# The last attention of a four-layer kernel: masking and exp in PSUM, probabilities as two 16-bit parts, turned by DMA instead of TensorE

## Chip, cores and metric

The kernel runs on one core of a Trainium2 chip. The metric is the time of one execution on the device in microseconds; the median of several runs is compared. TensorE, VectorE (DVE), ScalarE (ACT), GpSimd (POOL) and SyncE (SP) each work through an order of their own and wait for each other by semaphores. Every matmul writes to one of eight PSUM banks of 128 x 512 floats.

## What is computed

Four layers, each a cross attention and a feed-forward block with residuals, on x of 512 tokens by 512. The change touches only the attention of the last layer (B = 2 batches, 256 queries, 512 keys, 32 heads of 16 with 8 key groups, and a mask of true and false):

```python
def _L3_xattn_ref(q, k, v, w_q, w_k, w_v, w_out, mask):
    query = q @ w_q.T; key = k @ w_k.T; value = v @ w_v.T
    ...
    scores = jnp.einsum('bghnd,bgsd->bghns', query, key) / D_HEAD ** 0.5
    scores = jnp.where(mask, scores, jnp.finfo(scores.dtype).min)
    attention = jax.nn.softmax(scores, axis=-1)
    out = jnp.einsum('bghns,bgsd->bghnd', attention, value)
    return out.transpose(0, 3, 1, 2, 4).reshape(b, n, D_MODEL) @ w_out.T
x = x + _L3_xattn_ref(_layernorm(x), ctx_4096, ctx_4096, ..., mask_SxS2_bk0)
x = x + _L3_ffn_ref(_layernorm(x), ...)
```

## The kernel before

All arithmetic is to hold 32-bit accuracy, so operands are split into a high and a low part and multiplied part by part. The layers follow each other on every engine; layernorm ln6 leads into the last attention (`l3_...`), ln7 into the last feed-forward block (`f3_...`).

The last attention works on 128 tiles, each the scores of 128 queries against 512 keys for one head. `l3_tile(i)` gives a tile's block (four blocks of 32 tiles: batch and half of the heads), its head and its half of the queries; four tiles are a quad, and the two tiles of one head in a quad are a unit. The work is laid out in slots: slot k runs from -7 to 135, and each engine's function walks through the slots in the same order and does in slot k what is due there.

- TensorE (`l3_pe`): `scores` computes two tiles at a time (four matmuls, L1866) into the four banks `ring` (named ps_s in the profile); tile i has `ring[i % 4]`, and the bank is free when its mask is done (semaphore max). Two slots later `l3_pe` turns the tile's probabilities, four transposes of 128 x 128 (L1911), into `ps_t[0]` or `ps_t[1]` by turns; `take_turn_bank` waits until both parts of the piece before have left the bank. Turned values and turned reciprocals of the sums take turns in the same two banks; `pieces3` lists all pieces in order. `attend` (L1880) multiplies values and turned probabilities of a unit, eight matmuls, the unit's last tile four slots before. Projections (`l3_project`, `jobs3`) stand between them: a query job in 12 of the 32 quads, a key, value or output job in 10, none in 10. They use `ps_t[2]`.
- VectorE (`l3_dve`): in slot k `largest` adds the mask to tile k, takes the row maximum and writes the masked scores to SBUF (`l3p`, six buffers, L1995); then it forms the low part of the turned probabilities of tile k - 3 (L2019).
- ScalarE (`l3_act`): in slot k it copies the high part of the turned tile k - 3 (L1953), then takes exp of tile k in SBUF (L1962) with the row sums.
- GpSimd (`l3_pool`) splits weights, spreads reciprocals (L1789) and splits the attention's output (L1802, L1804).
- SP (`l3_sp`, `f3_sp`) issues the DMAs, each behind its wait, in one queue; in this stage only loads of weights, 8.4 MB.

```python
e.wait_ge(s3["exp"], i + 1)
for kk in range(4):
    mm = e.transpose(o[:, kk * P:(kk + 1) * P], l3p[:, i % 6, kk * P:(kk + 1) * P], ident[:, :])
mm.then_inc(s3["T"], 1)
```

The first attention (`L0`, class functions at L1220 to L1345) already works as the change does: masked scores and exp stay in PSUM (L1274, L1247), ScalarE writes a first 16-bit part (L1220), VectorE the second (L1315), and a DMA transpose turns both (L1071), one tile every 3.4 us.

## Time and profile before

| | |
|---|---|
| median of 3 runs | 1912.69 us (1910.24 to 1915.45) |
| the profiled execution, its own time | 1909.78 us |
| its span, first to last instruction | 1908.0 us |
| TensorE matmul, busy | 1752.3 us, 92% |
| TensorE weight load | 1419.0 us, 74% |
| VectorE | 1422.7 us, 75% |
| ScalarE | 1049.8 us, 55% |
| GpSimd | 882.7 us, 46% |
| mean granted TensorE clock | 0.972 of 2.4 GHz |
| DMA | 226.13 MB, mean 119 GB/s |

Busy shares are over the whole span, which has eight blocks with different limits; the last attention is its part from 1514 to about 1753 us. A line number names the operation in the code. In the groups, the time behind the bar is the idle time of the engine just before the operation, and behind it what ended most of that.

### The profile page before, as it was taken

To read this page: it belongs to the slowest core of one execution; us is meant where nothing else is said; L and a number is where in the kernel's file an instruction comes from. 1 tells how busy PE (TensorE), PEld (TensorE's weight loads), DVE (VectorE), ACT (ScalarE), POOL (GpSimd) and SP (SyncE) were. 2 spreads that over 40 slices of the span, in tenths; PEclk is the share of its full clock that TensorE was granted. 3 is DMA by queue.
4 is the path that set the end of the run, shared out by engine and by line. 5 is a ranking of instruction groups with operands and counts; after the bars stand their busy time and mean duration, and the time that the engine had idled before them with its cause. 6 is when DMAs were issued, how large, how long until landed. Compare 5 with 4: busy or idle time off the path is not lost.

```text
span 1908.0 us, 28955 instructions
## 1 busy us (share of the span) xinstructions
PE 1752.3 (92%) x9892; PEld 1419.0 (74%) x9892; DVE 1422.7 (75%) x3036; ACT 1049.8 (55%) x1999; POOL 882.7 (46%) x863
## 2 busy tenths in 40 slices
PE   6899999999797999978899999999988999998988
PEld 5677777777576888757688888888866778776755
DVE  6777887878577887747677777778755587787898
ACT  5766667666125565631556556656641287775333
POOL 6776776664633232044343444343336632242762
PEclk9999999999899999998999999999998999998998
DMA  5656656565417999651589778889762200120210
GB/s 183 142 103 139 134 116 141 121 120 118 121 25 141 213 194 175 136 121 50 108 159 196 160 166 175 164 162 194 149 141 78 75 1 23 46 90 22 73 44 23
DMA packets 524177, 226.13 MB, mean 119 GB/s; under 512 B 493696, under 2 KB 503168, under 8 KB 516736
## 3 DMA queue, kind: packets, MB, share of 16 engines
q1 hardware_dynamic: 524032, 224.28, 53.9%
q8 instruction: 81, 1.33, 0.3%
q14 instruction: 64, 0.52, 0.1%
HBM read 97.08 MB, written 5.24 MB: 54 GB/s over the span
## 4 chain that ended last, share of the span: by engine, by line
PE 69%; DVE 17%; DMA 3%; ACT 3%; issue 3%; POOL 3%; SPq 1%; POOLq 0%; DVEq 0%; ACTq 0%
PE ps_t L339 9%; PE ps_t L340 8%; PE ps_t L341 8%; PE ps_s L339 8%; PE ps_s L340 7%; PE ps_s L341 7%; PE ps_o L339 4%; PE ps_o L340 3%; PE ps_o L341 3%; PE ps_o L1880 3%; PE ps_t L1911 3%; ACT ps_s L1247 2%; PE ps_s L1866 2%; DVE nmax L1277 2%; DVE ps_s L1274 1%
## 5 line engine op out<-in xcount | busy, mean ns | idle before, releaser
L1247 ACT ACTIVATE ps_s<-ps_s,nmax 128x768 f32<-128x768 f32 (+1 forms) x320 | 252.6, 789 | 342.0 <-DVE nmax L1277 239.5
L1220 ACT ACTIVATE l_ab<-ps_s,rinv 128x768 f16<-128x768 f32 (+1 forms) x320 | 260.8, 815 | 69.0 <-DVE rinv L1322 54.1
L1315 DVE SCALAR_TENSOR_TENSOR l_ab<-ps_s,rinv,l_ab 128x768 f16<-128x768 f32 (+1 forms) x320 | 289.1, 903 | 2.8 <-ACT l_ab L1220 2.4
L1277 DVE TENSOR_REDUCE nmax<-ps_s 128x1 f32<-128x768 f32 x192 | 183.5, 956 | 123.3 <-PE ps_s L341 122.9
L339 PE MATMUL ps_o<-l_pt,l_v 128*128 128x256 f16 (+1 forms) x832 | 230.9, 278 | 19.3 <-DMA l_v<-l_vab 9.2
L340 PE MATMUL ps_o<-l_pt,l_v 128*128 128x256 f16 (+1 forms) x832 | 229.6, 276 | 0.0
L341 PE MATMUL ps_o<-l_pt,l_v 128*128 128x256 f16 (+1 forms) x832 | 229.5, 276 | 0.0
L339 PE MATMUL ps_s<-l_k_hi,l_q_hi 128*128 128x512 f32 (+3 forms) x512 | 186.4, 364 | 21.9 <-DVE l_ab L1315 18.9
L377 POOL TENSOR_TENSOR wo_hi<-raw_big,one 128x512 fp32r<-128x512 f32 (+2 forms) x100 | 103.8, 1038 | 204.6 <-PE ps_t L341 123.6
L340 PE MATMUL ps_s<-l_k_lo,l_q_hi 128*128 128x512 f32 (+3 forms) x512 | 179.8, 351 | 0.0
L341 PE MATMUL ps_s<-l_k_hi,l_q_lo 128*128 128x512 f32 (+3 forms) x512 | 179.1, 350 | 0.0
L377 POOL TENSOR_TENSOR wq_hi<-raw_big,one 128x512 fp32r<-128x512 f32 (+1 forms) x100 | 103.5, 1035 | 123.5 <-PE ps_t L341 59.2
L339 PEld LDWEIGHTS ps_s<-l_k_hi,l_q_hi 128*128 128x128 f32 (+1 forms) x512 | 96.4, 188 | 60.9 <-DVE l_ab L1315 32.2
L379 POOL TENSOR_TENSOR wq_lo<-raw_big,wq_hi 128x512 fp32r<-128x512 f32 (+1 forms) x100 | 127.5, 1275 | 7.8
L683 POOL TENSOR_TENSOR w_raw<-w_raw,w_row 128x512 f32<-128x512 f32 x32 | 41.1, 1285 | 191.4 <-DMA w_raw<-in_f_w 191.4
L2019 DVE TENSOR_TENSOR l_pt_lo<-ps_t,l_pt_hi 128x512 fp32r<-128x512 f32 x128 | 88.4, 691 | 48.2 <-ACT l_pt_hi L1953 45.5
L379 POOL TENSOR_TENSOR wo_lo<-raw_big,wo_hi 128x512 fp32r<-128x512 f32 (+2 forms) x100 | 120.7, 1207 | 7.8
L1274 DVE CUSTOM_DVE_ANT_0 ps_s<-ps_s,l_mask 128x512 f32<-128x512 f32 x128 | 88.7, 693 | 46.9 <-PE ps_s L341 46.9
L339 PEld LDWEIGHTS ps_o<-l_pt,l_v 128*128 128x128 f16 (+1 forms) x832 | 87.1, 105 | 48.0 <-issue 29.4
L339 PE MATMUL ps_t<-xT_hi,wq_hi 128*128 128x512 f32 (+1 forms) x296 | 117.1, 396 | 3.5 <-DVE xT_lo L2136 2.7
L340 PE MATMUL ps_t<-xT_lo,wq_hi 128*128 128x512 f32 (+1 forms) x296 | 110.9, 375 | 0.0
L341 PE MATMUL ps_t<-xT_hi,wq_lo 128*128 128x512 f32 (+1 forms) x296 | 110.7, 374 | 0.0
(386 smaller groups left out, 4947.0 us busy)
## 6 DMA issues: line engine op xcount, KB each, us to landing
raw_big<-in_l_wq SPq DMA_DIRECT2D x18, 1024.0 KB, 5.9
raw_big<-in_l_wo SPq DMA_DIRECT2D x18, 1024.0 KB, 5.9
w_raw<-in_f_w SPq DMA_DIRECT2D x32, 256.0 KB, 3.6
raw_big<-in_f_w SPq DMA_DIRECT2D x7, 1024.0 KB, 4.9
raw_kv<-in_l_wkv SPq DMA_DIRECT2D x12, 512.0 KB, 6.5
l_pt<-l_ab SPq DMA_TRANSPOSE x320, 3.7
raw_f<-in_f_w SPq DMA_DIRECT2D x4, 1024.0 KB, 4.8
w_nat<-in_f_w1n SPq DMA_DIRECT2D x16, 256.0 KB, 3.9
```

The costliest lines, as they stand in the source:

```text
L339: pe.matmul(o, a[0], b[0], start=start, stop=False)
L340: pe.matmul(o, a[0], b[1], start=False, stop=False)
L341: return pe.matmul(o, a[1], b[0], start=False, stop=stop)
L377: pool.tensor_tensor(hi, w, one[0:parts, 0:1].to_broadcast([parts, cols]), ALU.mult).then_inc(w_rdy[role], 1)
L379: pool.tensor_tensor(lo, w, hi.bitcast(F32), ALU.subtract).then_inc(w_rdy[role], 1)
L1220: e.activation(sp.ab[:, (k - 1) % 3, 0, :], self.scores_out(k - 1), ACT.Copy, scale=rinv[:, i:i + 1]).then_inc(s_pa, 1)
L1247: e.activation(self.scores_out(k), self.scores_out(k), ACT.Exp, bias=nmax[:, i:i + 1], scale=-1.0 if l.rope else 1.0, accum_out=rsum[:, i: ...
L1274: e.tensor_tensor_reduce(out=o, in0=o, in1=sp.mask[:, 2 * b + qt, :], scale=-1.0, scalar=F32_MAX, op0=ALU.add, op1=ALU.min, accum_out=nmax ...
L1277: e.tensor_reduce(nmax[:, i:i + 1], o, AX.X, ALU.max, negate=True).then_inc(s_max, 1)
L1315: e.scalar_tensor_tensor(out=b, in0=self.scores_out(t), scalar=rinv[:, i:i + 1], in1=a, op0=ALU.mult, op1=ALU.subtract).then_inc(s_pb, 1)
L1880: mm = e.matmul(ps_o[:, 0:SQ], l3v[blk % 2][:, k, g * P:(g + 1) * P], l3pt[u % 2][y][:, k, :], start=g == 0 and k == 0 and y == 0, stop=g ...
L2019: e.tensor_tensor(pt[1], ps_t[p % 2][:, :].rearrange("p (k q) -> p k q", q=P), pt[0].bitcast(F32), ALU.subtract).then_inc(s3["tlo"], 1)
```

## The change

- The masked scores and exp stay in the scores' PSUM banks; the mask writes in place. Scores now have five banks (`l3_bank`: the four of `ring` and `ps_t[0]`), and a bank is free when the second part of its tile is out.
- ScalarE copies the first 16-bit part of tile k right behind its exp in slot k, scaled by P_SCALE; VectorE forms the second part of tile k in slot k + 1. Both go to `l3ab`, six buffers of 128 x 1024 16-bit values.
- SP issues one `dma_start_transpose` per tile, 128 in all, into `l3pt`, six units. The transposes stand in SP's queue between the loads; the first loads of the next block move into this loop, behind tiles 71, 87 and 101. `l3ab[i % 6]` is free for tile i + 6 when its transpose has landed.
- `attend` waits for the transposes of its two tiles and runs three slots later; the steps behind it move three slots as well, and the stage ends at slot 138. The 32-bit transposes on TensorE are gone, and with them `take_turn_bank` and `pieces3`; values and reciprocals alone are turned there, in `ps_t[1]` (`take_aside`).
- The values are 16-bit in two parts too, scaled by their largest magnitude: a maximum, a diagonal, one more matmul, and five short operations per batch. The scale comes off with the reciprocals.
- Projection jobs inside quads start at the third slot of a quad, not the first.

```diff
-        l3pt = [[at(f"l3_pt{i}_{n}", [P, 4, SQ], F32R, R0 + 8 + 8 * i + 4 * j) for j, n in enumerate(("hi", "lo"))]
-                for i in range(2)]
-        l3p = at("l3_p", [P, 6, SK], F32, R0 + 24)
+        l3pt = [at(f"l3_pt{i}", [P, 2, 8, P], F16, R0 + 8 + 4 * i) for i in range(6)]
+        l3ab = [at(f"l3_ab{i}", [P, 2, SK], F16, R0 + kb) for i, kb in enumerate((66, 68, 70, 72, 32, 34))]
...
-                job(kind, blk, i, 4 * quad, 4 * quad, 4 * quad + 1, 4 * quad + 1)
+                job(kind, blk, i, 4 * quad + 2, 4 * quad + 2, 4 * quad + 3, 4 * quad + 3)
...
+        def l3_bank(i):
+            return (ring[0], ring[1], ring[2], ring[3], ps_t[0][:, :])[i % 5]
...
         def l3_sp(e):
-            load(e, "q", c3.q + 1, A["l3_wq"][1], ("o", c3.o + 1))
-            load(e, "o", c3.o + 1, A["l3_wo"][1], ("q", c3.q + 2))
+            for k in range(1, N3 + 1):
+                i = k - 1
+                u = l3_unit(i)
+                e.wait_ge(s3["second_part"], i + 1)
+                if u >= 6:
+                    e.wait_ge(s3["pv"], u - 5)
+                e.dma_start_transpose(l3pt[u % 6][:, l3_tile(i)[3], :, :], l3ab[i % 6][:, :, :].rearrange("p a n -> p (a n)"))\
+                    .then_inc(s3_crossed[i % 6], 16)
+                if k == 10:
+                    load(e, "q", c3.q + 1, A["l3_wq"][1], ("o", c3.o + 1))
+                if k == 40:
+                    load(e, "o", c3.o + 1, A["l3_wo"][1], ("q", c3.q + 2))
+                if k in F3_LOADS_AT:
+                    f3_sp_ahead(e, F3_LOADS_AT.index(k))
...
             def scores(quad, qt):
-                if quad:
-                    e.wait_ge(s3["max"], 4 * quad - 2 + 2 * qt)
+                pair = 2 * quad + qt
+                if pair >= 2:
+                    e.wait_ge(s3["second_part"], 2 * pair - 3)
...
             def attend(u):
-                e.wait_ge(s3["tlo"], lo_count3[piece_at3["t", u // 2 * 4 + 2 + u % 2]])
+                for i in (u // 2 * 4 + u % 2, u // 2 * 4 + u % 2 + 2):
+                    e.wait_ge(s3_crossed[i % 6], 16 * (i // 6 + 1))
...
-                if k % 4 >= 2 and 0 <= k - 6 < N3:
-                    attend((k - 6) // 4 * 2 + k % 2)
+                if k % 4 in (1, 2) and 0 <= k - 9 < N3:
+                    attend((k - 9) // 4 * 2 + (k - 1) % 4)
...
         def l3_act(e):
-                    e.activation(l3p[:, k % 6, :], l3p[:, k % 6, :], ACT.Exp, bias=nmax[:, c:c + 1], scale=-1.0,
-                                 accum_out=rsum[:, c:c + 1]).then_inc(s3["exp"], 1)
+                    o = l3_bank(k)
+                    e.activation(o, o, ACT.Exp, bias=nmax[:, c:c + 1], scale=-1.0, accum_out=rsum[:, c:c + 1]).then_inc(s3["exp"], 1)
+                    if k >= 6:
+                        e.wait_ge(s3_crossed[k % 6], 16 * (k // 6))
+                    e.wait_ge(s3["exp"], k + 1)
+                    e.activation(l3ab[k % 6][:, 0, :], o, ACT.Copy, scale=P_SCALE).then_inc(s3["first_part"], 1)
...
         def l3_dve(e, link):
+                if 0 <= k - 1 < N3:
+                    i = k - 1
+                    a, b = (l3ab[i % 6][:, part, :] for part in (0, 1))
+                    e.wait_ge(s3["first_part"], i + 1)
+                    e.scalar_tensor_tensor(out=b, in0=l3_bank(i), scalar=P_SCALE, in1=a, op0=ALU.mult, op1=ALU.subtract)\
+                        .then_inc(s3["second_part"], 1)
...
+        F3_LOADS_AT = (72, 88, 102)
+        def f3_sp_ahead(e, step):
+            if step == 0:
...
+                for i in range(2):
+                    e.dma_start(q_w1[i][:, :, :], w1_ints[:, 2 * i:2 * i + 2, :]).then_inc(s_wback[0], 16)
+            elif step == 1:
+                e.wait_ge(w_rdy["o"], 8 * cf.o)
+                f3_load_chunk(e, 0)
+                e.dma_start(q_w2[:, :, :], w2_ints).then_inc(s_wback[1], 16)
+            else:
+                e.wait_ge(w_rdy["q"], 8 * (cf.q + 1))
+                f3_load_chunk(e, 1)
```

TensorE in a quad with a query projection, before (ps_s and ps_t are banks, l_y keys, l_x queries, l_p the probabilities to be turned):

```order
L1911 MATMUL ps_t<-ident,l_p 128x128 x4
L1866 MATMUL ps_s<-l_y_hi,l_x_116 128x512
L1866 MATMUL ps_s<-l_y_lo,l_x_116 128x512
L1866 MATMUL ps_s<-l_y_hi,l_x_116 128x512
L1866 MATMUL ps_s<-l_y_lo,l_x_116 128x512
L339 MATMUL ps_t<-xT_hi,wq_hi 128x256
L340 MATMUL ps_t<-xT_lo,wq_hi 128x256
L341 MATMUL ps_t<-xT_hi,wq_lo 128x256
L339 MATMUL ps_t<-xT_hi,wq_hi 128x256
L340 MATMUL ps_t<-xT_lo,wq_hi 128x256
L341 MATMUL ps_t<-xT_hi,wq_lo 128x256
L1911 MATMUL ps_t<-ident,l_p 128x128 x4
```

and in the change, in a quad of the same kind, where l_pt are turned probabilities and l_v values:

```order
L1887 MATMUL ps_t<-l_y_hi,l_x_116 128x512
L1887 MATMUL ps_t<-l_y_lo,l_x_116 128x512
L1887 MATMUL ps_s<-l_y_hi,l_x_116 128x512
L1887 MATMUL ps_s<-l_y_lo,l_x_116 128x512
L1902 MATMUL ps_o<-l_pt_121,l_v_140 128x256 x8
L1887 MATMUL ps_s<-l_y_hi,l_x_116 128x512
L1887 MATMUL ps_s<-l_y_lo,l_x_116 128x512
L1887 MATMUL ps_s<-l_y_hi,l_x_116 128x512
L1887 MATMUL ps_s<-l_y_lo,l_x_116 128x512
L1902 MATMUL ps_o<-l_pt_122,l_v_140 128x256 x8
L345 MATMUL ps_t<-xT_hi,wq_hi 128x256
```

The transposes of l_p are gone from between the others, two scores of every five tiles in turn go to ps_t, and each quad has its two groups of products beside the scores.

ScalarE, before, with the semaphores that each row waits for:

```order
L1953 ACTIVATE l_pt_hi<-ps_t 128x4x128 [waits l3_pv,l3_T]
L1962 ACTIVATE l_p,rsum<-l_p,nmax 128x512 [waits l3_rec,l3_max]
L1953 ACTIVATE l_pt_hi<-ps_t 128x4x128 [waits l3_pv,l3_T]
L1926 ACTIVATE l_t<-ps_t,l_selq 128x256 [waits l3_job_out,l3_job_full]
L1962 ACTIVATE l_p,rsum<-l_p,nmax 128x512 [waits l3_rec,l3_max]
L1953 ACTIVATE l_pt_hi<-ps_t 128x4x128 [waits l3_pv,l3_T]
```

and in the change:

```order
L1976 ACTIVATE ps_s,rsum<-ps_s,nmax 128x512 [waits l3_rec,l3_max]
L1980 ACTIVATE l_ab_128<-ps_s 128x512 [waits l3_exp,l3_probs_crossed_5]
L1947 ACTIVATE l_t<-ps_t,l_selq 128x256 [waits l3_job_out,l3_job_full]
L1976 ACTIVATE ps_s,rsum<-ps_s,nmax 128x512 [waits l3_rec,l3_max]
L1980 ACTIVATE l_ab_123<-ps_s 128x512 [waits l3_exp,l3_probs_crossed_0]
```

The copy of a turned tile three slots back (L1953) has become the first part of the same tile, right behind its exp, and waits for that exp and for the transpose of six tiles before.

SP's queue in the change, around the loads behind tile 87; before, the two loads stood there alone:

```order
L1758 DMA_TRANSPOSE l_pt_117<-l_ab_125 128x8x128 [waits l3_pv,l3_second_part]
L1758 DMA_TRANSPOSE l_pt_118<-l_ab_126 128x8x128 [waits l3_pv,l3_second_part]
L2093 DMA raw_big<-in_f_w 128x2048 [waits w_o_split]
L2107 DMA q_w_189<-second_weight_rounded 128x8192
L1758 DMA_TRANSPOSE l_pt_119<-l_ab_127 128x8x128 [waits l3_pv,l3_second_part]
L1758 DMA_TRANSPOSE l_pt_120<-l_ab_128 128x8x128 [waits l3_pv,l3_second_part]
```

Each transpose waits for its tile's second part and for a unit's products; the loads stand in line between them.

## Rows read from the trace of the kernel before

**Rows 1.** Stretches: busy PE, PEld, DVE, ACT, POOL, clock, DMA share, GB/s
```profile
1634.00:1694.00 60.00, 58.83 (x428) 47.81 (x429) 47.69 (x117) 47.11 (x111) 24.97 (x31) 1.00 0.23 89
...
1742.00:1760.00 18.00, 14.61 (x84) 12.65 (x84) 8.49 (x18) 3.97 (x9) 3.37 (x6) 0.88 0.00 0
```

**Rows 2.** Chain that ended last, from 1505: start us, us, engine, tile, line
```profile
1562.33 0.66 PE ps_s L1866 x4
...
1568.47 0.66 PE ps_s L1866 x4
...
1604.99 0.66 PE ps_s L1866 x4
...
1611.96 0.67 PE ps_s L1866 x4
...
1615.16 0.44 PE ps_t L1911 x4
...
1649.20 0.66 PE ps_s L1866 x3
...
1657.55 0.66 PE ps_s L1866 x4
```

**Rows 3.** Groups by form, 1514 to 1738: busy us, mean ns, idle before
```profile
L2019 DVE TENSOR_TENSOR l_pt_lo<-ps_t,l_pt_hi 128x512 fp32r<-128x512 f32 x121 | 83.6, 691 | 44.6 <-ACT l_pt_hi L1953 42.0
...
L1953 ACT ACTIVATE l_pt_hi<-ps_t 128x512 fp32r<-128x512 f32 x121 | 72.0, 595 | 46.1 <-PE ps_t L1911 43.7
```

**Rows 4.** VectorE in order of time in the last attention
```profile
1653.68 0.69 DVE L2019 TENSOR_TENSOR l_pt_lo<-ps_t,l_pt_hi 128x512 fp32r<-128x512 f32 x1
1654.29 0.42 DVE L2034 TENSOR_TENSOR l_o<-ps_o,l_r 128x256 f32<-128x256 f32 x1
```

**Rows 5.** All engines in order of time, a tile of the first attention
```profile
231.93 0.70 DVE L1274 CUSTOM_DVE_ANT_0 ps_s<-ps_s,l_mask 128x512 f32<-128x512 f32 x1 [0.47 <-PE ps_s L341]
...
232.55 0.14 DVE L1274 DVE_READ_ACCUMULATOR2_ANT nmax<- 128x1 f32 x1
232.55 0.75 DVE L1315 SCALAR_TENSOR_TENSOR l_ab<-ps_s,rinv,l_ab 128x512 f16<-128x512 f32 x1
...
232.73 0.66 ACT L1247 ACTIVATE ps_s<-ps_s,nmax 128x512 f32<-128x512 f32 x1 [1.45 <-DVE nmax L1274]
...
233.31 0.19 ACT L1247 ACTIVATION_READ_ACCUMULATOR ps_s<-ps_s,nmax 128x1 f32 x1
```

**Rows 6.** Groups by form, ScalarE, whole span
```profile
L1220 ACT ACTIVATE l_ab<-ps_s,rinv 128x512 f16<-128x512 f32 x128 | 87.7, 685 | 17.6 <-DVE rinv L1322 14.7 <-DMA l_pt<-l_ab 0.3
```

**Rows 7.** ScalarE in order of time: a pair whose second waits for the first
```profile
1886.20 0.63 ACT L2283 ACTIVATE q_c<-q_c 128x512 f32<-128x512 f32 x1 [2.81 <-DVE q_c L2376]
1886.86 0.63 ACT L2285 ACTIVATE hq<-q_c 128x512 bf16<-128x512 f32 x1
```

**Rows 8.** DMA queues, 420 to 440: packets, MB, share of 16 engines
```profile
q1 hardware_dynamic: 5784, 1.44, 37.4%
```

**Rows 9.** The transposes of the first attention, 100 to 300: issue and landing
```profile
L1071 SPq DMA_TRANSPOSE l_pt<-l_ab x55: 1231/1232/2171, 101.2 to 298.0; - x55
...
DMA to landing us min/median/max: 3.0/3.0/6.8
```

**Rows 10.** DMA queues, 1300 to 1350
```profile
DMA packets 24957, 8.71 MB, mean 174 GB/s; under 512 B 23672, under 2 KB 24312, under 8 KB 24825
...
q1 hardware_dynamic: 24953, 8.65, 88.3%
```

**Rows 11.** DMA queues, 1514 to 1742, the last attention
```profile
q1 hardware_dynamic: 1152, 8.40, 10.0%
```

**Rows 12.** VectorE in order of time: the last mask, the last scaling
```profile
1742.40 0.68 DVE L1995 CUSTOM_DVE_ANT_0 l_p<-ps_s,l_mask 128x512 f32<-128x512 f32 x1
...
1751.31 0.42 DVE L2034 TENSOR_TENSOR l_o<-ps_o,l_r 128x256 f32<-128x256 f32 x1 [2.00 <-PE ps_o L1880]
```

More of the change, by code:

```diff
@@ L1654, in program @@
         c3 = START["l3"]
-        s3 = {n: sem(f"l3_{n}") for n in ("S", "max", "exp", "rec", "T", "thi", "tlo", "pv", "spread", "scaled", "ohi", "olo", "zero", "sel",
+        s3 = {n: sem(f"l3_{n}") for n in ("S", "max", "exp", "first_part", "second_part", "rec", "aside", "aside_free", "vhi",
+                                         "vdiag", "vscale", "pv", "spread", "scaled", "ohi", "olo", "zero", "sel",
                                          "job_full", "job_hi", "job_out")}
+        s3_crossed = [sem(f"l3_probs_crossed_{i}") for i in range(6)]
         N3 = 4 * 32
@@ L1704, in program @@
         find3 = {(j.kind, j.blk, j.i): j for j in jobs3}
-        slots3 = range(-7, 136)
+        slots3 = range(-7, 139)
         steps3, ended3 = {}, {}
@@ L1811, in l3_project @@
                 e.wait_ge(s3["job_out"], {4: 0, 5: 1, L3_JOBS - 1: j.n - 1}.get(j.n, j.n) or 1)
+            if part == 0 and j.n == L3_JOBS - 1:
+                e.wait_ge(s3["second_part"], N3)
             o = j.bank()
@@ L1928, in l3_act @@
             e.wait_ge(s3["sel"], 1)
-            e.wait_ge(s3["zero"], 2)
+            e.wait_ge(s3["zero"], 3)
             job_out(jobs3[0])
@@ L2003, in l3_dve @@
             for k in slots3:
[L2004 removed]
+                if k == 124:
                     norms[7].dve_scale(e, 0)
```

180 lines of the change are left out of this document (86 added, 94 removed).

## Prediction

> **What bounds the kernel now.** I read the slices of the page first, then busy time by stretch, the chain of waits, the groups, and the engines in order of time where the change cuts in. The last attention takes its 128 tiles, by the first and last mask, from 1514.6 to 1742.4: 228 us, 1.78 us a tile, 7.12 us a quad (four tiles).
>
> In a stretch of 60 us TensorE is busy 58.8 us at its full clock of 2.4 GHz, VectorE 47.7, ScalarE 47.1, the DMA engines 23% with loads [rows 1]. The chain is TensorE's line after line, and it dates the quads: from one first pair of scores to the next it is 6.14 us in a quad without a projection, 6.97 with a query projection, 8.35 with a key, value or output projection [rows 2]. The program has 10, 12 and 10 of these: 61.4 + 83.6 + 83.5 = 228.5 us, the whole stage. VectorE and ScalarE stand idle before the two parts of the turned probabilities, 44.6 and 46.1 us in all, for each other and for TensorE's turn [rows 3]. So TensorE's order is the bound, with a good fifth of the other two free.
>
> **What goes.** The 128 groups of four TensorE transposes cost 0.44 us each on the chain [rows 2]: 128 x 0.44 = 56 us, 1.76 a quad. Left on TensorE: 4.4, 5.2 and 6.6 us by kind of quad, 172 us in all. The 16-bit products stream as many columns as the 32-bit ones; I give them no gain.
>
> **What takes its place: the loop of ScalarE and VectorE.** VectorE masks tile k and then forms the second part of tile k-1; ScalarE takes exp of k and then the first part of k. That closes a loop over two tiles: second part of k-1, mask of k+1, exp of k+1, first part of k+1, second part of k+1. Its steps, where all is ready: second part to the next operation 0.61 [rows 4]; mask to the end of its accumulator read 0.76 (231.93 to 232.69), to exp 0.04, exp to the end of its read 0.77 [rows 5]; the wait of ScalarE for itself 0.03 [rows 7]; the first part 0.60, which is the old copy out of PSUM [rows 3] (0.69 if it behaves as the first attention's, which takes its factor from memory [rows 6]; the new factor is a constant, so I take 0.60); to VectorE 0.03. Sum 2.84 us (2.93), so 1.42 a tile, 5.7 a quad. Neither engine alone is slower than that: VectorE needs 0.62 + 0.61 = 1.23 a tile, and exp with its read, wait and copy 1.40 on ScalarE.
>
> Beside these run keys, queries, scales and residuals. Today they make up what is left of VectorE's time: 47.7 us over 33.7 tiles is 1.42, less 1.23 is 0.19 a tile [rows 1, 4, 5]; for ScalarE I estimate half of that, 0.10, by its narrower copies. Put wholly into the loop they give 1.71 a tile (219 us), wholly absorbed 1.42 (182). Two such loops run interleaved, of the odd and the even tiles, and an operation put into one delays the other less, by what is left of the slack between the engines' 1.23 and 1.40 and the loop's 1.42; that is little, so I take 0.21 of the 0.29: 1.63 a tile, **209 us**, against 228: **-19**. Heavy quads need 6.6 us of TensorE against 6.5 of the loop: even, no term.
>
> **The DMA engines.** Now 128 transposes of 256 KB pass them. In a stretch with nothing else 5784 packets took 37.4% of 20 us; one transpose is 1024 packets of 256 bytes, so 7.48 / 5.65 = 1.32 us each [rows 8]. The stage's own loads, 8.40 MB, took 10.0% of 228 us, 22.8 us, 2.7 us a MB [rows 11]. Together 169 + 23 = 192 us of 209: hidden on average, but 92% full. Issue takes 1.23 us of SP's queue per transpose, landing 3.0 [rows 9]; 1.23 is under 1.63, so the queue keeps up.
>
> What it costs are the loads that sit in the same queue ahead of transposes: 2 MB behind tile 71, 3 MB behind tile 87, 1 MB behind 9, 39 and 101. The first part of tile k waits until tile k-6 has crossed. From the end of the second part of k-6 to that point are six tiles less the 2.2 us from its exp to that end, plus 0.8 to the copy: 9.8 - 2.2 + 0.8 = 8.4 us, 5.4 more than the landing takes. 1 MB (2.7 us) and 2 MB (5.4) fit, 3 MB (8.1) leave 2.7 us; with SP held at tile 101 by POOL's splitting of the query weights I take **+4**. The products on TensorE tolerate more (a unit is taken three slots later, about 10 us behind its last second part). If the cover were gone, each transpose would show its 3.0 us of landing at once: 384 us.
>
> The Trainium skill (DMA: Bandwidth & Descriptors, Latency and other measured facts) gives a DMA transpose 261 GB/s, an estimated 1.0 us for 256 KB, by which the engines would be some 150 us busy and no stall would be left; the trace gives 1.32, and that is used.
>
> **Small edits.** At the start VectorE gets a maximum over the values and five short scale operations between query results, partly beside TensorE: +1 (0 to 2). At the end the last mask starts at 1742.40 and the last scaling at 1751.31, 8.9 us [rows 12]. The new path from the last mask is 0.80, 0.77, 0.63 and 0.03, second part 0.7, landing 3.0, one product group 0.95: 6.9, plus queue delay of perhaps 1: -1 (-2 to +3). The new masks write PSUM: 0.70 for 0.68, in the steps above. Smaller zero fills on POOL lie ahead of everything: nothing.
>
> **Sum.** -19 + 4 + 1 - 1 = -15 us. The profiled execution took 1909.8 us; the median of the runs is 1912.7, 2.9 more. 1912.7 - 15 = 1897.7, so **1898 us**.
>
> **Rivals.**
> *The DMA engines become the bound, and it is slower.* Where transposes and loads are dense, they take longer: 88.3% of 50 us, less 7.0 us for 2.59 MB that were not transposes (8.65 MB less 23672 packets of 256 bytes), is 37.1 us for 23.1 units of 1024 packets, 1.61 each [rows 10]. Then the stage is 128 x 1.61 + 22.8 = 229 us, plus some 4 us before the first transpose can start and 5 of backlog behind the last mask: +8, **1921 us**. It decides from (209 - 22.8) / 128 = 1.45 us per transpose on, and is slower than before from about 1.54. For it: the load is denser than anywhere in the first attention. Against: much of the busy time in such stretches is packets waiting for each other, and the bare cost was 1.32. Chance 0.18.
>
> The Trainium skill (VectorE: DVE Perf Modes, The three transpose paths) speaks against the change in the same way, and harder: a 128 x 128 block 1309 ns by DMA against 390 ns on TensorE. Eight blocks one after the other would be an estimated 10.5 us per tile, 1340 us for the stage. The trace doesn't agree, since a transpose of eight blocks lands in 3.0 us.
>
> *Half a gain.* First part at 0.69, extras wholly in the loop and 4 us more of stalls: 1.76 a tile, 225 us: -3 + 4 = about +1, **1913 us**. VectorE's wait times support it, the length of six buffers speaks against the stalls. Chance 0.14.
>
> *More than forecast.* Extras absorbed: 1.45 a tile is 186 us, under the DMA floor of 192, so about 195 us: -33, **1880 us**. Chance 0.08.
>
> *The clock falls* between TensorE's bursts: it was 0.88 of 2.4 GHz on average where it ran thin at the end of the stage [rows 1]. At 1.2 GHz a plain quad would take 8.8 us, 2 more than now forecast; but the new gaps are under 1 us, and the low stretch had one of 3. Within the next case's width; chance 0.03, +3 us.
>
> **Numbers.** My case, 1885 to 1906 us, has 0.57; it makes nearly all of faster. Differences over 0.3% (5.7 us) can be told from none. Faster 0.67, within 0.3% 0.16, slower 0.17. The range takes in the absorbed extras and most of the DMA case: 1882 to 1920.
>
> **What would show it.** Right: TensorE 75 to 85% busy in the stage; VectorE's idle time before the second part waiting for ScalarE, hardly for TensorE; transposes landing in 3 to 5 us, a few ScalarE copies waiting for a transpose near tile 93; DMA share 0.9. Wrong: landing times that grow through the whole stage and a share of 1.0 throughout (the DMA case), or a tile over 1.75 us with short landings (the loop).

## The result and the profile after

The change makes the kernel slower: 1926.05 us median of 4 runs (1925.10 to 1928.26) against 1913.53 us of 4 runs of the kernel before (1910.24 to 1915.45) on the same chip. The ratio is 1.0070, 95% interval 1.0053 to 1.0088: **+12.5 us**, where 1898 us was forecast (1882 to 1920). The first row of each of the next two views is the stretch from the last low part of the turned layernorm ahead of the stage (`xT_lo`) to the first one of the block behind it.

Busy time by stretch, the kernel before (length; PE, PEld, DVE, ACT, POOL; clock, DMA share, GB/s):

```profile
1506.62:1762.74 256.12, 242.13 (x1676) 195.22 (x1674) 196.39 (x474) 183.22 (x428) 75.55 (x107) 0.98 0.10 35
```

The same, the changed kernel, and four stretches of 20 us inside it:

```profile
1512.45:1780.06 267.61, 211.30 (x1168) 143.59 (x1166) 208.99 (x489) 185.56 (x428) 74.08 (x107) 0.82 0.82 158
...
1554.00:1574.00 20.00, 16.11 (x121) 11.59 (x120) 18.61 (x47) 18.24 (x45) 4.11 (x8) 1.00 1.12 183
1574.00:1594.00 20.00, 15.54 (x78) 9.89 (x78) 14.46 (x33) 14.03 (x33) 11.14 (x12) 0.74 0.81 154
...
1594.00:1614.00 20.00, 17.56 (x83) 11.54 (x83) 15.42 (x36) 14.14 (x33) 2.35 (x5) 0.74 0.94 182
...
1694.00:1714.00 20.00, 14.17 (x72) 8.79 (x70) 14.64 (x35) 14.24 (x34) 11.11 (x12) 0.71 1.05 221
```

The stage is 11.5 us longer, which is most of the 12.5. (The two profiled executions themselves lie 18.5 us apart, 1928.26 and 1909.78: 5.8 us of that are ahead of the stage and 1.1 behind it. The stage begins anywhere from 1506.3 to 1516.1 in the profiled executions of the changed kernels below, whose work ahead of it is the same, so the 5.8 are taken for scatter.) TensorE's mean granted clock there went from 0.98 to 0.82 of 2.4 GHz. The clock has two levels, 1.0 and 0.5, so 0.18 / 0.5 = 36% of the stage, 96 us, ran at 1.2 GHz; before it was some 10 us. Where the clock stayed at 1.00 (1554 to 1574), VectorE and ScalarE are busy 18.6 and 18.2 of 20 us: that is the loop of the forecast. Where it was 0.71 to 0.74 they are busy 14 to 15. The DMA share adds up packet times and reaches 1.12 here, so 1.0 is not its ceiling.

Where the 11.5 us lie (times from VectorE in order of time):

| part | before | changed | forecast of the difference |
|---|---|---|---|
| last `xT_lo` to the first mask | 8.0 | 11.3 (+3.3) | +1 |
| first to last mask (127 tiles on) | 227.8 | 235.2 (+7.4) | -15 |
| last mask to the next block's `xT_lo` | 20.3 | 21.2 (+0.8) | -1 |

**The operations cost what was forecast.** Groups by form of the changed kernel, 1514 to 1745 (busy us, mean ns, idle before and its releasers):

```profile
L2033 DVE SCALAR_TENSOR_TENSOR l_ab<-ps_s,l_ab 128x512 f16<-128x512 f32 x95 | 65.6, 691 | 11.2 <-ACT l_ab L1980 10.1
L1976 ACT ACTIVATE ps_s<-ps_s,nmax 128x512 f32<-128x512 f32 x96 | 63.5, 662 | 18.9 <-PE ps_t L347 11.4 <-DVE nmax L2016 5.6
L1980 ACT ACTIVATE l_ab<-ps_s 128x512 f16<-128x512 f32 x95 | 56.7, 597 | 8.4
```

Second part 691 ns, exp 662, first part 597 (I took 0.60). The surprise is the releaser of exp: a projection's last matmul (`ps_t L347`).

**The quads give it away.** From the first mask of a quad to that of the next there are 31 intervals. A projection's result is taken by ScalarE and VectorE at the start of the quad behind it, so ten intervals hold a key, value or output result: the 2nd, 3rd, 10th, 12th, 13th, 18th, 20th, 21st, 28th and 30th. They take 10.2, 8.4, 12.0, 10.5, 6.5, 8.3, 10.3, 6.5, 9.6 and 10.3 us (rounded), 92.6 in all. At my 1.63 a tile they would be 65.2. The 24th (9.7) and the 26th (9.1) stand beside the 3 MB of loads and GpSimd's splitting of the query weights; the other 19 take 119.6, 6.3 each, *less* than the 6.5 of the forecast. My 1.63 a tile and 4 us of stalls make 211 us of the 127 tiles from first to last mask; it took 235.2. Of these 24 us, 27.4 are in the ten intervals, 1.8 in the loads' two beyond the 4 I had given them, and the rest came out 5 better. Part of the ten is no wait at all: VectorE alone is busy 67.6 us in them, 6.8 each, since the work on a projection's result falls on these quads and I had spread it evenly over all tiles.

What one of them looks like, the 10th, 1585.3 to 1597.3. The changed kernel in order of time, PE and ACT and DVE rows only:

```profile
1584.75 1.91 PE L1902 MATMUL ps_o<-l_pt,l_v 128*128 128x256 f16 x8
...
1586.31 0.77 PE L345 MATMUL ps_t<-cT_hi,wkv_hi 128*128 128x512 f32 x1
...
1590.59 0.40 PE L347 MATMUL ps_t<-cT_hi,wkv_lo 128*128 128x512 f32 x1
...
1591.02 0.60 ACT L1943 ACTIVATE l_y_hi<-ps_t 128x512 fp32r<-128x512 f32 x1 [4.29 <-PE ps_t L347]
...
1591.65 0.69 DVE L1987 TENSOR_TENSOR l_y_lo<-ps_t,l_y_hi 128x512 fp32r<-128x512 f32 x1 [4.20 <-ACT l_y_hi L1943]
...
1591.98 1.05 PE L1902 MATMUL ps_o<-l_pt,l_v 128*128 128x256 f16 x8
```

And its clock, busy time by stretch of the changed kernel:

```profile
1573.00:1576.00 3.00, 2.00 (x16) 1.15 (x14) 2.72 (x7) 2.72 (x8) 0.00 (x0) 1.00 1.01 193
1576.00:1579.00 3.00, 1.71 (x12) 1.03 (x12) 2.79 (x7) 2.75 (x7) 0.00 (x0) 1.00 1.02 190
1579.00:1585.00 6.00, 4.64 (x20) 2.42 (x21) 5.59 (x15) 4.94 (x13) 5.17 (x7) 0.56 0.98 188
1585.00:1591.00 6.00, 6.00 (x22) 4.37 (x20) 1.72 (x4) 1.64 (x4) 5.77 (x6) 0.59 0.86 164
1591.00:1597.00 6.00, 3.74 (x28) 2.26 (x28) 5.14 (x12) 5.54 (x13) 0.20 (x1) 0.98 0.43 26
```

TensorE was busy 1.7 to 2.0 of 3 us in plain quads, then the clock fell to 1.2 GHz. Eight products took 1.91 us in place of 1.05; TensorE waited 0.54 us for the spread reciprocals of GpSimd; the key projection ran from 1586.31 to 1590.99, 4.7 us. (The projection's last three matmuls, from 1590.13 on, are at full clock again.) Its result is due in ScalarE's queue ahead of the next exp, and in VectorE's ahead of the next mask: both stood still for over 4 us (busy 1.6 and 1.7 of 6). Meanwhile TensorE worked without a gap and the clock came back. The Trainium skill (TensorE: Matmul & The Clock Gate, A second HAM failure mode: psum-queue depth-cycling) tells of such an oscillation where TensorE idles briefly and often between groups of matmuls; this trace agrees, and the gaps are short ones here too (rows of them stand in the section on the prediction).

All such waits of ScalarE and VectorE, the changed kernel, 1514 to 1750 and 1516 to 1760 (engine, line, waited for: us in total, times, longest):

```profile
ACT ps_s L1976 <- PE ps_t L347: 11.4, 5, 3.9
ACT l_y_hi L1943 <- PE ps_t L347: 8.4, 3, 4.3
ACT ps_t L1976 <- PE ps_t L347: 6.8, 2, 4.1
...
ACT l_ab L1980 <- DMA l_pt<-l_ab: 3.1, 1, 3.1
...
DVE l_ab L2033 <- ACT l_ab L1980: 17.7, 54, 3.0
DVE x L2006 <- PE ps_t L347: 10.4, 4, 3.4
```

26.6 us of ScalarE go to ten projection results, and one wait of 3.1 to a landing.

**The DMA engines** are nearly full, as forecast, and it hardly shows. The transposes of the changed kernel, 1516 to 1760 (issue min/median/max ns; landing us; queue):

```profile
L1758 SPq DMA_TRANSPOSE l_pt<-l_ab x126: 1231/1276/6016, 1526.7 to 1759.0; - x126
...
DMA to landing us min/median/max: 3.0/3.3/10.8
...
q1 hardware_dynamic: 133004, 41.15, 87.4%
```

**The start.** The changed kernel in order of time, the operations that the scale of the values brought:

```profile
1515.30 0.68 DVE L1996 TENSOR_REDUCE l_vmax<-ps_s 128x1 f32<-128x512 f32 x1
1516.02 0.69 DVE L1997 COPY l_vs<-ps_s 128x512 f32<-128x512 f32 x1
1516.63 0.35 DVE L2000 TENSOR_SCALAR l_diag<-ident,l_vmax 128x128 f32<-128x128 f32 x1
1516.80 0.47 ACT L1947 ACTIVATE l_t<-ps_s,l_selq 128x256 fp32r<-128x256 f32 x1 [2.42 <-DVE l_vs L1997]
...
1517.04 0.49 PE L1922 MATMUL ps_t<-l_diag,l_ones 128*128 128x128 f32 x2 [1.81 <-DVE l_diag L2000]
```

The maximum and the diagonal hold TensorE for 1.8 us in the middle of the query projections, and the clock drops behind it. In fill_matmuls below, with the same instructions up to here and the same wait, the clock stays at 1.00 and this part takes 9.8 us in place of 11.3: 1.8 us are the wait and 1.5 the clock. **The end**, the changed kernel, VectorE:

```profile
1758.88 0.69 DVE L2016 CUSTOM_DVE_ANT_0 ps_s<-ps_s,l_mask 128x512 f32<-128x512 f32 x1
...
1769.13 0.48 DVE L2065 SCALAR_TENSOR_TENSOR l_o<-ps_o,l_vout_scale,l_r 128x256 f32<-128x256 f32 x1 [7.17 <-PE ps_o L1902]
```

10.3 us from the last mask to the last scaling, against 8.9 [rows 12].

### The profile page after: what moved, and what is told of

Same layout as the page of the kernel before. It is cut to its first block, busy times and chain, and to the rows that moved or that the text cites. A ratio compares the mean times of both kernels' runs of the same rounds, so it can differ in the third digit from the quotient of the medians.

```text
span 1926.5 us, 28003 instructions
## 1 busy us (share of the span) xinstructions
PE 1729.1 (90%) x9384; PEld 1373.7 (71%) x9384; DVE 1433.8 (74%) x3050; ACT 1051.4 (55%) x1999; POOL 880.6 (46%) x864
## 4 chain that ended last, share of the span: by engine, by line
PE 61%; DVE 18%; ACT 6%; POOL 5%; DMA 4%; issue 4%; SPq 2%; ACTq 0%; POOLq 0%; DVEq 0%
PE ps_t L345 8%; PE ps_t L346 8%; PE ps_t L347 8%; PE ps_s L345 8%; PE ps_s L347 7%; PE ps_s L346 7%; PE ps_o L345 3%; PE ps_o L346 3%; PE ps_o L347 3%; ACT ps_s L1253 2%; DVE nmax L1283 1%; PE ps_o L1902 1%; DVE ps_s L1280 1%; DVE l_ab L2033 1%; DVE l_k_lo L1005 1%
## 5 line engine op out<-in xcount | busy, mean ns | idle before, releaser
L347 PE MATMUL ps_o<-l_pt,l_v 128*128 128x256 f16 (+1 forms) x832 | 230.9, 278 | 0.0
L347 PE MATMUL ps_s<-l_k_hi,l_q_lo 128*128 128x512 f32 (+3 forms) x512 | 179.7, 351 | 0.0
L347 PE MATMUL ps_t<-xT_hi,wq_lo 128*128 128x512 f32 (+1 forms) x296 | 112.0, 378 | 0.0
L346 PEld LDWEIGHTS ps_s<-l_k_lo,l_q_hi 128*128 128x128 f32 (+1 forms) x512 | 96.9, 189 | 17.2
```

Of the source, the lines that this page charges most:

```text
L346: pe.matmul(o, a[0], b[1], start=False, stop=False)
L347: return pe.matmul(o, a[1], b[0], start=False, stop=stop)
```

## The experiments

Three theories. **Clock**: with the transposes gone TensorE has gaps, the granted clock falls, and at 1.2 GHz TensorE is the bound again. **Blocked queues**: the results of the heavy projections (key, value, output) come too late for their place in ScalarE's and VectorE's orders. **DMA**: transposes and loads contend. Each run was compared with the kernel before on the same chip; the ratio is to that. The changed kernel's own is 1.0070.

| run | median us | ratio, 95% interval | stage us | clock | ten heavy intervals us |
|---|---|---|---|---|---|
| changed kernel | 1926.05 | 1.0070 (1.0053 to 1.0088) | 267.6 | 0.82 | 92.6 |
| fill_matmuls | 1916.71 | 1.0020 (1.0010 to 1.0029) | 257.2 | 0.93 | 81.1 |
| fill_transposes | 1914.88 | 1.0011 (0.9994 to 1.0028) | 256.3 | 0.95 | 81.0 |
| jobs_spread | 1916.53 | 1.0024 (1.0009 to 1.0039) | 257.1 | 0.86 | 78.0 |
| start_later | 1926.38 | 1.0062 (1.0039 to 1.0084) | 266.8 | 0.81 | 93.5 |
| outputs_later | 1922.01 | 1.0039 (1.0025 to 1.0054) | 262.7 | 0.83 | 86.7 |
| loads_apart | 1926.34 | 1.0066 (1.0047 to 1.0085) | 269.6 | 0.81 | 93.9 |
| half_crossing | 1927.26 | 1.0067 (1.0052 to 1.0082) | 267.1 | 0.83 | 90.7 |
| four_edits | 1910.02 | 0.9983 (0.9972 to 0.9993) | 251.9 | 0.93 | 77.1 |
| placed_filled | 1907.11 | 0.9967 (0.9955 to 0.9979) | 249.1 | 0.94 | 76.0 |
| placed_unfilled | 1910.94 | 0.9988 (0.9978 to 0.9998) | 251.5 | 0.87 | 77.2 |
| placed_tuned | 1905.07 | 0.9963 (0.9947 to 0.9979) | 249.6 | 0.92 | 75.9 |
| placed_half_crossing | 1899.47 | 0.9943 (0.9928 to 0.9959) | 242.4 | 0.94 | 75.7 |

Stage, clock and intervals are of the profiled run of each, the stage between the same two points as above (before: 256.1 us and 0.98). A profiled run can lie 5 us from the median of its kernel (fill_transposes: 1909.29 against 1914.88), so the medians decide and the stages say where. Against the kernel before, the medians of the changed kernels come out 0 to 3 us worse than their stages do; where these lie is open.

### TensorE's gaps filled: fill_matmuls and fill_transposes

```diff
+        FILL = 4
...
+            def fill(k, n):
...
+                e.wait_ge(s3["aside_free"], count)
+                for _ in range(n // (4 if k // 4 in HEAVY else 2 if k // 4 in QUERY else 1)):
+                    e.matmul(aside_bank[:, 0:SQ], l3ones[:, :].bitcast(F16)[:, 0:P], l3ones[:, :].bitcast(F16)[:, 0:SQ], start=True, stop=True)
...
             for k in slots3:
+                if k % 4 in (0, 1, 2):
+                    fill(k, FILL)
...
                 if k % 4 == 1 and 0 <= k + 3 < N3:
+                    fill(k, FILL)
                     scores((k + 3) // 4, 0)
```

In the second run the matmul is `e.transpose(aside_bank[:, 0:P], ident[:, :], ident[:, :])`.

> The changed kernel with 241 matmuls of 128 x 256 16-bit values added to TensorE's order in the last attention, into the bank for turned values at times when it is free; nobody reads them. Full clock: 0.11 us each, 26 us of work in all; four before each of four waits in a quad without projection, two in a query quad, one in a heavy quad. Clock theory (gaps in TensorE's work let the granted clock fall, and at 1.2 GHz TensorE is the bound again): the clock of the stage, 0.82 on average in the changed kernel, comes back above 0.93, the stage gets 12 to 25 us shorter although TensorE has more to do, time 1901 to 1914 us. DMA theory (contention of transposes and loads sets the tile): the filling changes nothing, 1926 us, or more. Order theory (TensorE's own order is the bound, whatever the clock): up to 26 us longer, 1935 to 1950.

> The same places and the same number, 241, but each a TensorE transpose of 128 x 128 32-bit values (0.11 us each by the old kernel's 0.44 for four) in place of a matmul. If transposes hold the clock like matmuls: the same as the run with matmuls, 1901 to 1914 us. If they don't: the clock stays near 0.82 and the time near 1926 or some us above. The kernel before had 512 such transposes in this stage and a clock of 0.99, so I expect the first.

Measured: 1916.71 and 1914.88 us, 9 to 11 us less than the changed kernel, with *more* work for TensorE. Busy time by stretch over the stage, fill_matmuls:

```profile
1511.18:1768.36 257.18, 213.65 (x1409) 151.04 (x1407) 207.56 (x488) 185.14 (x428) 74.63 (x107) 0.93 0.86 165
```

and fill_transposes:

```profile
1506.28:1762.53 256.25, 212.81 (x1409) 156.90 (x1407) 207.56 (x489) 185.15 (x428) 74.70 (x107) 0.95 0.87 165
```

The clock is back at 0.93 and 0.95. The two runs agree interval by interval within 0.3 us, so between real matmuls an added 32-bit transpose holds the clock as well as an added matmul. Whether transposes alone would, no run shows. The Trainium skill (TensorE: Matmul & The Clock Gate, Part 4: PE-mode transpose) says that transposes do not count as busy for the full clock in the same way; these two runs don't agree with it, as far as 32-bit transposes among matmuls go. By parts of the stage: the start is 1.5 us shorter (no filler stands there, so that much of the gain isn't the fillers'), first to last mask 11.7 shorter, the end 2.7 longer. The time landed 3 and 1 us above the forecast band of the clock theory, so the clock is a true cause and not the whole: the ten heavy intervals fell only to 81 us, at a clock of 0.97 in them (0.85 in the changed kernel). Four of them (the 12th, 18th, 20th and 30th) lie in stretches of 20 us whose clock was 1.00 throughout, and still took 7.4 to 8.8 us. The 24th interval, by the 3 MB of loads, went the other way, from 9.7 to 11.9, and ScalarE's waits for landings from 3.1 to 8.2 us: a loop that gets there sooner seems to run into that stall. One cost of the filling is plain too: from the last mask to the next block it takes 23.9 us for 21.2, since fillers stand in the last slots as well.

### The parts of a projection spread: jobs_spread

```diff
-                job(kind, blk, i, 4 * quad + 2, 4 * quad + 2, 4 * quad + 3, 4 * quad + 3)
+                job(kind, blk, i, 4 * quad, 4 * quad + 1, 4 * quad + 2, 4 * quad + 3)
```

> The changed kernel with the four parts of a projection job in the four slots of its quad, one in each, not two in the third and two in the fourth. No work is added. Clock theory: TensorE's work is more even within heavy and query quads, so fewer falls there, but the plain quads keep theirs: clock 0.85 to 0.90, 4 to 10 us shorter, 1916 to 1922. DMA theory: 1926. Order theory: the products of a unit and the scores wait less behind a job's burst, 2 to 5 us shorter.

Measured 1916.53 us, 9.5 less, just inside the clock theory's band. ScalarE's waits of jobs_spread, 1514 to 1750:

```profile
ACT ps_s L1976 <- PE ps_t L347: 2.2, 4, 0.6
ACT l_y_hi L1943 <- PE ps_t L347: 1.3, 3, 0.5
ACT ps_t L1976 <- PE ps_t L347: 0.5, 1, 0.5
```

What went are the waits for projection results, from 26.6 us to 4.0, and the ten heavy intervals fell by 14.6 us; the other 19 grew by 2.8. The stage's clock rose only from 0.82 to 0.86, but in the ten intervals it rose from 0.85 to 0.94: the low clock moved to where it costs little. So this run doesn't part the two causes by itself. Next to fill_matmuls it does in part: that run has more clock in the ten (0.97) and late projections, and they take 81.1 us, 3 more than here. The edit does two things, it spreads the parts and it starts them two slots earlier; the key projection of the 10th interval started at 1575.60 and was done ahead of 1582.70, at full clock all through; these two effects are not parted either. Of all single edits this one moves the heavy intervals most. So near full clock the late start of the projections costs some 3 us of its own (5 by placed_filled against fill_matmuls, below), and more where the clock is low.

The 20th interval shows how little the place can do at full clock; the changed kernel, fill_matmuls, jobs_spread and placed_filled (below), in this order, busy time by stretch:

```profile
1661.41:1671.74 10.33, 9.60 (x47) 6.92 (x46) 6.51 (x16) 5.89 (x15) 0.00 (x0) 0.83 1.11 267
```

```profile
1649.23:1658.07 8.84, 8.45 (x50) 6.00 (x49) 6.51 (x16) 5.62 (x14) 0.00 (x0) 1.00 1.12 279
```

```profile
1650.16:1659.10 8.94, 8.57 (x51) 5.70 (x50) 6.42 (x16) 6.21 (x15) 0.00 (x0) 1.00 1.12 279
```

```profile
1648.22:1656.65 8.43, 8.04 (x51) 5.58 (x49) 6.36 (x15) 6.91 (x16) 0.00 (x0) 1.00 1.15 216
```

At full clock it takes 8.4 to 8.9 us wherever the projection starts, with TensorE busy for all but 0.4 of them.

### Results taken later: outputs_later

```diff
+        outputs3 = {}
+        for j in jobs3:
+            outputs3.setdefault(j.end + 1 + (j.kind != "q" and 0 <= j.end < N3), []).append(j)
...
-                for j in ended3.get(k - 1, ()):
+                for j in outputs3.get(k, ()):
```

> The changed kernel with the results of the ten key, value and output projections that lie inside quads taken by ScalarE and VectorE one slot later (after the tile of the second slot behind the job's last part, not the first). Theory of the blocked queues: in the changed kernel ScalarE waits 26.6 us for TensorE's projection results ahead of exp (10 waits of 1.9 to 4.3 us) and VectorE behind it; one slot of 1.5 us more takes 10 x 1.5 to 10 x 2.5 off, 10 to 20 us shorter, 1906 to 1916 us, and since TensorE goes on working meanwhile, the clock rises a little too. Clock theory alone: the heavy quads are long since TensorE works at 1.2 GHz there; the wait only moves to the scores, 0 to 4 us shorter. DMA theory: 1926.

Measured 1922.01 us, 4 less (6 by the two ratios, whose intervals just meet). That is outside the band of the blocked queues, and what was recorded for the clock theory alone: 0 to 4 less, since the wait only moves. ScalarE's waits of outputs_later, 1514 to 1750:

```profile
ACT l_v L1962 <- PE ps_t L1919: 8.4, 4, 3.8
ACT l_ab L1983 <- DMA l_pt<-l_ab: 8.1, 5, 5.5
ACT ps_s L1979 <- PE ps_t L347: 7.6, 3, 2.8
```

The waits for projections fell from 26.6 to 7.6 us, and 8.0 more for the turned values and 5.0 more for landings took their place. Its waits for VectorE's maxima grew by 4.3 as well (10.9 for 6.6). The reading that fits, not tested by itself, is that while TensorE works off a late projection at 1.2 GHz, everything behind it is late too, whoever takes its result. My expectation had counted the wait and not what is next in TensorE's queue.

### Start and loads: start_later and loads_apart

```diff
-            for at_k, piece in ((-5, ("max", 0)), (6, ("max", 1))):
+            for at_k, piece in ((2, ("max", 0)), (6, ("max", 1))):
...
+                if k == 0:
+                    e.wait_ge(s3["job_out"], 2)
+                    link(e.tensor_reduce(l3vmax[:, 0:1], l3vs[:, 0, :], AX.X, ALU.max, apply_absolute_value=True))
+                    e.tensor_scalar(l3diag[:, :], ident[:, :], l3vmax[:, 0:1], None, ALU.mult).then_inc(s3["vdiag"], 1)
```

```diff
-        F3_LOADS_AT = (72, 88, 102)
+        F3_LOADS_AT = (72, 77, 88, 94, 104)
```

> The changed kernel with the largest value, the diagonal and the scale of batch 0 taken after the first mask and not between the query results. If these operations cost the start what I read in the trace (12.3 us from the turned layernorm's end to the first scores, against 9.0 before): 3 us shorter, 1923. If only the falling clock stretched the start, 1 us or nothing. The stage behind is not touched by either theory.

> The changed kernel with the loads of 2 MB behind tile 71 and 3 MB behind tile 87 taken apart: 1, 1, 1, 2 and 1 MB behind tiles 71, 76, 87, 93 and 103. What I forecast as a stall of 4 us, and the trace of the changed kernel shows as one wait of 3.1 us of ScalarE for a transpose, goes: 2 to 4 us shorter, 1922 to 1924. If that stall were hidden behind the slow quads anyway: 1926.

Measured 1926.38 and 1926.34 us, for 1923 and 1922 to 1924 expected: neither is told from the changed kernel. Both did locally what they should. In start_later the stretch to the first mask fell from 11.3 to 8.0 us, the value of before, which prices the scale operations with the clock behind them at 3.3; but the first interval took 0.8 more (the maximum now stands in the loop), and the 28th rose from 9.6 to 11.1, so the masks took 237.0 in place of 235.2 us. In loads_apart the 24th interval fell from 9.7 to 6.9, the 26th rose from 9.1 to 11.0 and the 28th from 9.6 to 11.1. At the 26th TensorE and ScalarE waited for the spread reciprocals, which stood in GpSimd's queue behind a wait for a projection. Waits of loads_apart, 1695 to 1712:

```profile
POOL wq_hi L383 <- PE ps_t L347: 12.9, 1, 12.9
...
PE ps_t L1928 <- POOL l_rb L1810: 3.7, 1, 3.7
ACT l_r L1967 <- PE ps_t L1928: 3.0, 1, 3.0
```

### The DMA theory: half_crossing

```diff
-                e.dma_start_transpose(l3pt[u % 6][:, l3_tile(i)[3], :, :], l3ab[i % 6][:, :, :].rearrange("p a n -> p (a n)"))\
+                e.dma_start_transpose(l3pt[u % 6][:, l3_tile(i)[3], 0:4, :], l3ab[i % 6][:, 0, :])\
...
-                                      l3pt[u % 6][:, :, 4 * y + k, :],
+                                      l3pt[u % 6][:, :, k, :],
```

> The changed kernel with only the first 16-bit part turned by DMA (128 KB a tile in place of 256), and the product taking that part twice, so that the second part is left out of the result; ScalarE, VectorE and TensorE do the same work as in the changed kernel. DMA theory (transposes and loads contend for the engines and set the tile): 10 to 20 us shorter, 1906 to 1916, the share of the DMA engines in the stage near 0.5. Clock theory and theory of the blocked queues: only the stall of 3 us and part of the end, 0.5 to 1.5 us, go: 1921 to 1924.

This kernel leaves the second parts of the probabilities out of its result; it is there for its time alone. Measured 1927.26 us, no gain, not even the small one that the other two theories had left for it (1921 to 1924). Over the stage, half_crossing:

```profile
1513.07:1780.15 267.08, 209.31 (x1168) 143.64 (x1166) 208.98 (x488) 185.83 (x428) 74.22 (x107) 0.83 0.45 96
```

The DMA share falls from 0.82 to 0.45 and the stage stays at 267. The DMA engines don't set the changed kernel's time; that theory falls for this kernel.

### Put together: four_edits, placed_filled, placed_unfilled

```diff
-                job(kind, blk, i, 4 * quad + 2, 4 * quad + 2, 4 * quad + 3, 4 * quad + 3)
+                job(kind, blk, i, *[4 * quad + a for a in ((2, 2, 3, 3) if kind == "q" else (1, 1, 2, 3))])
...
-                if 33 <= k < 37:
-                    split(e, "q", c3.q + 1, None, k - 33)
+                if 34 <= k < 38:
+                    split(e, "q", c3.q + 1, None, k - 34)
...
-                if 96 <= k < 100:
-                    split(e, "q", c3.q + 2, None, k - 96)
+                if 98 <= k < 102:
+                    split(e, "q", c3.q + 2, None, k - 98)
...
-        F3_LOADS_AT = (72, 88, 102)
+        F3_LOADS_AT = (72, 78, 88, 94, 100, 108)
```

The diff is of the two placed kernels, beside the filling (in one of them), the later results and the later scale.

> The changed kernel with four edits at once: the 241 filling matmuls, results of heavy projections one slot later (their four parts in slots 1, 2, 3, 3 of the quad in place of 2, 2, 3, 3), the loads apart, the scale of batch 0 after the first mask. If clock, blocked queues and loads are the causes and separate: from 1926, 10 + 12 + 5 + 2 less, 1893 to 1902 us, the quads with key, value and output projections under 7.5 us each at a clock of 1.00, which is the loop I had forecast. If something else takes its place (the DMA engines, 128 x 1.5 us and 23 of loads = 215): no better than 1905.

> The four edits as before (with the filling matmuls), and three more: the parts of a key, value or output projection one slot to one and a half earlier (slots 1, 1, 2, 3 of the quad, its result taken two slots after the last part as in the four edits); the last 2 MB load in two halves of 1 MB, six ticks or more between any two loads; GpSimd's splits of the query weights begin one or two slots later, behind the spreading of the reciprocals. Theory of the blocked queues plus clock: the intervals between first masks that hold such a projection, 6.4 to 10.2 us with the four edits (11.9 where the 2 MB load stood), fall to 6.0 to 7.5, 10 to 14 us shorter in all: 1896 to 1902 us, clock of the stage 0.97 or more. If the DMA engines now set the tile (share 1.0 to 1.1 already): landing times that grow through the stage, and 1905 to 1910.

> The same without the 241 filling matmuls. Clock theory: the gaps of TensorE are back, the clock falls to half in a third of the stage, and although nothing else differs the time is 6 to 12 us longer than with them: 1904 to 1912. If only the blocked queues mattered, and the clock fell because of those stalls: within 3 us of the filled one.

Measured 1910.02, 1907.11 and 1910.94 us: all three are faster than the kernel before. The first two fall short of their main bands by 8 and 5 us and land in what was recorded for DMA engines that take over as the limit (no better than 1905; 1905 to 1910). The unfilled one stands inside its band. The stage of placed_filled and of placed_unfilled:

```profile
1515.13:1764.19 249.06, 212.17 (x1409) 148.48 (x1407) 206.12 (x489) 184.77 (x428) 74.69 (x107) 0.94 0.91 170
```

```profile
1514.12:1765.59 251.47, 199.71 (x1168) 135.13 (x1166) 207.63 (x488) 185.13 (x428) 74.18 (x107) 0.87 0.89 168
```

With the projections in time, the filling is worth 3.8 us (the intervals of the two ratios just meet; 6 to 12 expected), where it was worth 9.3 in the changed kernel. The low clock costs most where a projection is already late; both causes work through the same wait. The ten heavy intervals say the same four ways: 92.6 us late and unfilled, 81.1 filled, 77.2 placed earlier, 76.0 with both. (The placed kernels also have the later results, the later scale and the loads apart, so the 77.2 is not the place alone.) ScalarE and VectorE no longer wait for a key, value or output projection at all. What is left, ScalarE's waits of placed_filled, 1514 to 1750:

```profile
ACT ps_s L1994 <- DVE nmax L2035: 17.4, 24, 2.2
ACT l_ab L1998 <- DMA l_pt<-l_ab: 7.8, 6, 2.8
```

The ten intervals stand at 76.0 us, not at 65. VectorE alone is busy 65.9 us in them, so no more than 10 us are left to reach; those I haven't split, beyond the 20th interval shown above. The DMA share is 1.06 between 1550 and 1740, and ScalarE waits for six landings, 7.8 us in all.

### The next bound: placed_tuned and placed_half_crossing

placed_tuned is placed_filled with the first value projection's result back at its old place and the loads behind tiles 71, 79, 89, 99, 109 and 119; placed_half_crossing is placed_filled with the two edits of half_crossing.

> The filled kernel with the earlier placed projections, and two more edits: the value projection of the first quad gives its result one slot after its last part as in the changed kernel (TensorE waited 2.6 us for it before the key projection), and the six loads of about 1 MB stand ten tiles apart, behind tiles 71, 79, 89, 99, 109 and 119. Expected: 2 us less in the second quad and 2 to 4 us of the waits for landings around tiles 96 to 110, so 1901 to 1904 us. If the DMA engines, now busy 97% of the stage, set the tile by themselves, the waits only move to other tiles: 1906 or 1907 as before.

> The filled kernel with the earlier placed projections (not the tuned one), with only the first 16-bit part turned and the product taking it twice, so that the second part is left out of the result; the engines do the same work. With half the crossing the DMA engines are busy half of the stage. If they are by now the next limit: 5 to 10 us shorter than the same kernel with the full crossing, 1897 to 1902 us. If VectorE and ScalarE's loop and the remaining waits for TensorE are the limit: 0 to 3 us shorter, 1904 to 1907, the waits of ScalarE for a landing (7.8 us) gone, but taken up elsewhere.

Measured 1905.07 and 1899.47 us, for 1901 to 1904 and 1897 to 1902 expected. The tuned kernel is the fastest complete one, 0.37% (0.21 to 0.53) under the kernel before, but its interval does not part it from placed_filled. Halving the crossing, worth nothing in the changed kernel, is worth 7.6 us here by the medians on two chips, 4.6 by the two ratios; against placed_tuned, on the same chip, it is 5.6. The stage of placed_half_crossing:

```profile
1510.29:1752.72 242.43, 211.06 (x1409) 148.58 (x1407) 206.16 (x488) 184.93 (x428) 74.70 (x107) 0.94 0.52 106
```

So with the other two out of the way the crossing is the next limit, but not all through the stage. The first 21 intervals take 139.9 us in placed_filled and 140.0 here; all of the difference is in the last ten, beside the loads of the next block, most in the 26th (9.7 to 7.6) and the 27th (8.5 to 5.8). ScalarE's waits for landings, 7.8 us, are gone. So it is transposes and loads together that cost here, and the transposes alone set no tile. In this kernel the first to the last mask takes 211.4 us, against the 211.0 that my 1.63 a tile and 4 for stalls make of 127 tiles: the forecast's stage exists, but only with late projections, low clock and half of the crossing out of the way, and by other terms (19 intervals at 6.2, ten at 7.6).

## Why the prediction was wrong

**Right, with numbers.** The durations: second part 0.69, exp 0.66, first part 0.60. The loop: 6.3 us in the 19 undisturbed intervals, where 6.5 was taken. The transposes on TensorE gone: its busy time in the stage fell from 242.1 to 211.3 us, though much of the latter was at half clock. The DMA engines full on average and hidden: shown by half_crossing. The stall behind the 3 MB load, near tile 93: one wait of 3.1 us, 4 taken; with luck, since in the kernels with a faster loop it was more (ScalarE's waits for landings 8.0 to 8.2 us in fill_matmuls, jobs_spread and outputs_later).

**The step that failed first** was "Heavy quads need 6.6 us of TensorE against 6.5 of the loop: even, no term." It compared two sums over a quad and left out where in the quad the work lies. (It also set the loop's 6.5 for them, where VectorE alone is busy 6.8.) The change moved the projections to the third and fourth slot, with the result due at the head of the next quad. In those two slots of 1.6 us each TensorE has one unit of products, 0.95, and the whole projection, twelve matmuls at steps of 0.23 (1583.45 to 1583.67 in fill_matmuls), 2.7 at full clock: 3.7 us for 3.3, nothing to spare, and at 1.2 GHz, with steps of 0.43 and 1.9 for the products, 7.1 (6.2 in the 10th interval, 1584.75 to 1590.99, with the end at full clock). Each microsecond over that stands in front of exp *and* of the mask. Measured: +27.4 us in ten intervals in place of no term. jobs_spread, a change of four numbers, took 14.6 off it, with the clock back in these intervals; holding the clock alone took 11.5 off. Either takes about half of it, and both together 16.6 (placed_filled), so this step and the next one failed together.

**The second was the rival of the clock**, at chance 0.03 and +3 us, because "the new gaps are under 1 us, and the low stretch had one of 3". The gaps are longer than that. TensorE's waits of the changed kernel, 1524 to 1757:

```profile
PE ps_s L1887 <- DVE l_ab L2033: 28.5, 27, 1.9
PE ps_t L1887 <- DVE l_ab L2033: 11.4, 10, 2.5
```

1.1 us on average and 2.5 at the most; none has 3 us, and the clock fell all the same. Measured by the filling, the clock is worth some 9.3 us in this kernel, 1.5 of it at the start where no filler stands. And the rival was priced on plain quads, 2 us each; the cost came in the heavy ones, through the late results.

**The start** was +3.3 for +1: I put the scale's operations "partly beside TensorE", but the matmul that waits for the diagonal stands in TensorE's queue ahead of two query projections, so TensorE's wait of 1.8 us and the clock behind it came on top. **The end** was +0.8 for -1, within the bounds given.

**The DMA rival**, at 0.18, gave a time of 1921 that is near the measured one by luck, for the wrong reason: the landings had a median of 3.3 us and half the crossing changed nothing. (Its own terms, 229 for 228 and 4 and 5, make +10 and 1923, not +8.) Its price shows only in the placed kernels. **The signs** failed too: TensorE was 79% busy in the stage, inside the 75 to 85 that were to show the forecast right, because much of it ran at half clock; and 1.85 us a tile with short landings was to put the blame on the loop, which ran at 6.3 us per undisturbed quad. None of the signs was on the clock.

What stays open: how the gains of start_later and loads_apart were lost in detail. No run held the clock fixed while these alone were changed. No run held it fixed either while the projections alone were moved, so what their place costs at full clock (3 to 5 us) is an estimate from runs that differ in more than that. A filling that leaves the last slots free, by the end times worth some 2 us, was not tried.
